# Attention weights' subtraction from GpSimd to VectorE, and later in the order

## The reference

```python
P = X @ W_in + b_in                     # 16 heads, each with Q, K, V, G of 64 columns
W = jnp.power(EPS + _cdist(Q, K), -2)   # EPS = 1e-4; _cdist: square root of the squared distance
W = W / (EPS + jnp.sum(W, axis=-1, keepdims=True))
A = jnp.einsum('hbts,hbse->hbte', W, V)
H = G * A                               # then @ W_out + b_out, residual, layer norm, sign-weight layer
```

## Time and profile before

| | |
|---|---|
| median of two runs | 5235.52 us (5234.5 to 5236.54) |
| profiled execution | 5237.27 us |
| its span on the slowest core | 5235.7 us |
| spans of the 8 cores | 5224.2 to 5235.7 us |
| first subtraction to the last | 347.2 to 4882.3 us |
| busy: PE, DVE, ACT, POOL | 52%, 24%, 58%, 42% of the span |
| mean granted TensorE clock | 0.653 of 2.4 GHz |

### The profile page before, as it was taken

The page is one execution under the profiler, slowest core; times in us unless marked ns, Lnnn a source line. Parts: engine busy times, 40 slices in busy tenths (PEclk is TensorE's granted clock), DMA queues, the critical chain, the costliest instruction groups (busy, mean ns, idle before and its releaser), DMA issues.

```text
span 5235.7 us, 45463 instructions; the slowest of 8 cores (5224.2 to 5235.7 us)
## 1 busy us (share of the span) xinstructions
PE 2736.5 (52%) x11472; PEld 1069.2 (20%) x11472; DVE 1273.1 (24%) x2118; ACT 3059.5 (58%) x2321; POOL 2176.6 (42%) x716
## 2 busy tenths in 40 slices
PE   1165555555555555546555555555465555544435
PEld 1122121212212121212122121212121221211112
DVE  4431312122121313131212213131312122120144
ACT  2127576675757575766667575757667675767200
POOL 0025444454545454444545354544445453545100
PEclk9976666666665656656666666666666666655657
DMA  2200000000000000000000000000000000000211
GB/s 77 63 7 1 9 2 6 5 1 9 2 9 1 9 2 10 1 7 3 2 9 1 9 2 9 1 9 2 7 4 1 9 2 9 1 1 1 97 32 65
DMA packets 42920, 64.15 MB, mean 12 GB/s; under 512 B 12992, under 2 KB 31424, under 8 KB 41664
## 3 DMA queue, kind: packets, MB, share of 16 engines
q1 hardware_dynamic: 36288, 61.03, 3.8%
q0 software_dynamic: 6400, 0.22, 0.1%
HBM read 50.39 MB, written 8.39 MB: 11 GB/s over the span
## 4 chain that ended last, share of the span: by engine, by line
PE 28%; POOL 25%; ACT 18%; issue 12%; DVE 9%; DMA 6%; DVEq 0%; POOLq 0%; SPq 0%; ACTq 0%
POOL wb L503 25%; PE pA L517 10%; ACT Ebc L498 9%; PE pp L333 8%; PE pS L480 5%; ACT Lb L489 5%; DMA Wst<-w_in 2%; DVE Wbf L318 2%; ACT Ea L495 2%; DMA rsrow<-A_sb 2%; DVE k2row L402 1%; PE pS L836 1%; PE pp L364 1%; PE pS L682 1%; PE pp L398 1%
## 5 line engine op out<-in xcount | busy, mean ns | idle before, releaser
L503 POOL TENSOR_TENSOR wb<-Ea,Ebc 128x2048 bf16<-128x2048 f32 x512 | 2080.9, 4064 | 2026.4 <-ACT Ebc L498 1634.8
L489 ACT ACTIVATE Lb<-pS 128x1024 f32<-128x1024 f32 x1024 | 1016.3, 1016 | 1093.5 <-PE pS L480 1090.9
L517 PE MATMUL pA<-wb,Vs 128*65 128x512 bf16 x2048 | 810.9, 538 | 1515.8 <-POOL wb L503 1515.8
L498 ACT ACTIVATE Ebc<-Lb 128x2048 bf16<-128x2048 f32 x512 | 972.7, 1900 | 92.9 <-POOL wb L503 92.0
L495 ACT ACTIVATE Ea<-Lb 128x2048 f32<-128x2048 f32 x512 | 977.8, 1910 | 77.3 <-ACT Lb L489 3.4
L480 PE MATMUL pS<-Qaug,Kaug 66*128 66x512 bf16 x2048 | 907.2, 546 | 213.8 <-ACT Lb L489 125.5
L517 PEld LDWEIGHTS pA<-wb,Vs 128*65 128x65 bf16 x2048 | 281.5, 138 | 2025.0 <-issue 1974.0
L333 PE MATMUL pp<-XnT,Wbf 128*64 128x512 bf16 x2048 | 598.5, 446 | 168.7 <-DVE Wbf L318 168.7
L371 DVE CAST Vs<-pp 128x64 bf16<-128x64 f32 x512 | 112.2, 224 | 1481.2 <-PE pp L364 1479.7
L364 PEld LDWEIGHTS pp<-Wbf,XnT 128*128 128x128 bf16 x4096 | 294.6, 130 | 240.1 <-issue 227.2
L333 PEld LDWEIGHTS pp<-XnT,Wbf 128*64 128x64 bf16 x2048 | 235.9, 125 | 521.6 <-issue 401.4
(11 more groups left out here) (83 smaller groups left out, 1164.3 us busy)
## 6 DMA issues: line engine op xcount, KB each, us to landing
xst<-x SPq DMA_DIRECT2D x32, 512.0 KB, 3.6
Wst<-w_in SPq DMA_DIRECT2D x128, 128.0 KB, 2.2
XT<-xT SPq DMA_DIRECT2D x8, 1024.0 KB, 16.9
y<-XT SPq DMA_DIRECT2D x32, 256.0 KB, 2.5
wst<-w_out SPq DMA_DIRECT2D x8, 512.0 KB, 4.5
wst<-w_ffn SPq DMA_DIRECT2D x8, 512.0 KB, 3.7
Kaug<-k2row POOLq DMA_DIRECT2D x128, 1.0 KB, 1.5
H<-Htmp SPq DMA_DIRECT2D x32, 64.0 KB, 1.9
```

The lines of the kernel that those rows point to most:

```text
L489: st("scalar", lambda e, ps=ps, sb=(r // 2) % 2, half=r % 2: e.activation(out=Lb[sb][:, half * 1024:half * 1024 + 1024], in_=pS[ps][:], fu ...
L498: st("scalar", lambda e, s=s: e.activation(out=Ebc[:], in_=Lb[s % 2][:], func=AF.Exp, scale=-1.5, bias=LN2EPS), waits=[(s_c3, s)], inc=s_c2)
L503: st("gpsimd", lambda e, s=s: e.tensor_tensor(out=wb[s % 2][:], in0=Ea[s % 2][:], in1=Ebc[:], op=ALU.subtract), waits=[(s_c2, 2 * s + 2), ...
L517: st("tensor", lambda e, hb=hb, stile=stile, ws=s % 2, half=r % 2, k=k, bk=bk: e.matmul(pAb[bk][0:65, :], Vs[hb][:, stile * 65:stile * 65 ...
```

## The change

The subtraction is given to VectorE instead of GpSimd, and it is emitted later in the region: behind the splice of the projection group (and behind A, the epilogue and `flush_w`) instead of right behind the exponentials. Operands, waits and semaphores stay as they are. It is emitted before the scores that open a new head.

```diff
     def emit_c3(s):
-        st("gpsimd", lambda e, s=s: e.tensor_tensor(
+        st("vector", lambda e, s=s: e.tensor_tensor(
             out=wb[s % 2][:], in0=Ea[s % 2][:], in1=Ebc[:], op=ALU.subtract),
            waits=[(s_c2, 2 * s + 2), (s_wcons, max(0, 4 * s - 4))], inc=s_c3)
...
         emit_c1(r)
         if r % 2 == 1:
             emit_c24(r // 2)
-            emit_c3(r // 2)
...
         if slot_in_head == 0:
             flush_w()
         splice(slot_in_head + 1, NQC * NREG)
+        if r % 2 == 1:
+            emit_c3(r // 2)
         if r + 1 < NTOT and nxt_head_start:
             emit_S(r + 1)
```

## The result

The changed kernel takes 5162.9 us (median of 7 runs, 5157.9 to 5179.5) where the kernel before takes 5235.6: a ratio of 0.986, 95% interval 0.984 to 0.987. That is 73 us, clear of noise and within the 2% that the forecast called no change. The profiled execution has a span of 5161.9 us on its slowest core.

A forecast was written before the change was run, and what follows sets the result against it. No engine is full; a loop of hand-overs sets the pace. Per head -9.0 + 8.8 + 1.8 + 1.9 - 2.7 = +0.8, 15 heads +12; last head -27.9, final subtraction -1.7: total -17.6, 5218, put at 5220 us (5090 to 5330).

The forecast's parts named there:

- The subtraction's price: One 2048-element subtraction on VectorE: 2.29 us, bounded by 2.04 and 2.42; with hand-over 2.56 instead of 4.22.
- V pairs: Region pairs 7 to 23 with V projection groups: 6.27 us each; eight with an epilogue 56.7 against 61.2, -9.0 a head.
- The epilogue's VectorE work: T1b and H, costed at nothing as hidden beside A and the first group; uncovered, 1.5 us in 60 pairs, 90 us.
- Wide pairs: Pairs 1 to 6 (Q, K) and 25 (G): most gaps cost one slow group, 10.2 us each, about 8.5 before.
- Norm pairs: Pairs 27 to 31, with square-and-row groups: 9.1 us each, five 45.5 against 43.6, +1.9 a head.
- The DMA behind the subtraction: Last pair to next head's scores: 2.3 us, or 4.2 if the DMA issue waits for the subtraction; 3.3 taken, -2.7.
- The head's start: Scores to pair 8: casts end 5.0 us earlier, but the first subtraction waits behind them; 106.5 against 97.7, +8.8.
- The last head: No projection groups, so ScalarE's floor sets most pairs: 200.4 us against 228.3, -27.9.
- head 0 behaves like the others: Head 0 has no wait for its successor's weights before or after, and loses the same in its wide groups.
- stay up: Rival: shorter TensorE gaps keep the clock high, seven wide pairs at 8.66 us, 180 us in all: 5040; chance 0.18.
- fall for whole pairs: Rival: one gap per pair keeps both groups and A at 1.2 GHz, wide pairs 12.8 us: 5475; chance 0.14.
- Face value: Rival: queue order costs nothing, so the subtraction's chain share shrinks by 572 us: 4660; chance 0.08, including cases between.

The follow-up runs named there:

- the early subtraction: Against the kernel before, the subtraction moved to VectorE but still emitted right behind the exponentials, ahead of the second group's evacuation: 4880.0 us, ratio 0.932.

## Why the prediction was right

The forecast was 5220 us, 5090 to 5330, within 2% at 0.64; measured were 5162.9 and -1.4%. The sum was 57 us too high: it forecast 15 us of gain and 73 came. Both lie under the 105 us that count as no change, so that the forecast held says little by itself, and the size of the gain was not foreseen. What bears the mechanism out are the steps:

**The subtraction's price.** Forecast 2.29 us, measured 2291 ns in 512 instructions. The bounds of 2.04 and 2.42 were not needed. The figure of the Trainium skill, "VectorE: DVE Perf Modes", The perf-mode tier table, 2293 ns for fp32, is met although one input is bf16.

**V pairs.** Forecast 56.7 us for eight, measured 56.3. Single ones are mostly 5.7 (the floor) or 6.3, and the pair with an epilogue is 13.2 to 13.5 on the mean (forecast 13.3). The epilogue's VectorE work, put at nothing, was next to nothing: the pair behind it takes 6.4.

**Wide pairs.** Forecast 10.2, measured 10.2, and more evenly than I thought: not "most gaps cost one slow group" but all except one of the 75 intervals from pair 1 to pair 6. Where the V pairs follow (6 to 7), the clock is still up and the pair takes 5.6 instead of 6.3; pair 25 is 11.1 instead of 10.4, as A is slow as well.

**Norm pairs.** Forecast 9.1, measured 9.1 to 9.3 (46.1 for five), link by link (columns as in the earlier trace rows):

```profile
2284.23 2.29 DVE L503 TENSOR_TENSOR wb<-Ea,Ebc 128x2048 bf16<-128x2048 f32 x1 [0.34 <-DVE k2row L402]
2284.59 1.91 ACT L495 ACTIVATE Ea<-Lb 128x2048 f32<-128x2048 f32 x1
2284.66 0.48 POOL L407 DMA_DIRECT2D Kaug<-k2row  x1 [2.57 <-DVEq L302]
2286.44 0.41 DVE L390 TENSOR_TENSOR KQsq<-Kaug 64x512 bf16<-64x512 bf16 x1
...
2289.24 0.68 DVE L402 CAST k2row<-pp 1x512 bf16<-1x512 f32 x1 [2.39 <-PE pp L398]
...
2292.30 0.68 DVE L402 CAST k2row<-pp 1x512 bf16<-1x512 f32 x1 [1.69 <-DMA Kaug<-k2row]
...
2293.31 2.29 DVE L503 TENSOR_TENSOR wb<-Ea,Ebc 128x2048 bf16<-128x2048 f32 x1 [0.34 <-DVE k2row L402]
```

**The DMA behind the subtraction.** I left open whether GpSimd can issue a DMA while VectorE subtracts, and took the middle of 2.3 and 4.2 us. The third row above settles it: issued at 2284.66 in 0.48 us, in the midst of the subtraction (2284.23 to 2286.52). So it is for 90 of the 192 row DMAs: their issues, 0.48 us each, lie within a subtraction, and the rows land 1.56 us (median) after the start of the issue, against 1.52 for the others. At the end of a head the scores came 2.1 us after the subtraction's start (2313.66 against 2311.60 and 2595.82 against 2593.72, both below). The middle was 1.2 us a head too high. The rule of the Trainium skill, "SBUF — State Buffer", SBUF: two separate sides, names for instructions with two SBUF inputs only a conflict with GpSimd instructions that read SBUF; I had stretched it to descriptor writes, and this trace does not bear that out. Nor are the casts of the earlier trace rows, with one input each, a case of two inputs; the squares (L390) are: 75 of 192 took over 1 us before, each beside a GpSimd subtraction, and none does now.

**The head's start: the term that was mis-sized.** I read it at head 8 and took it for all heads. There are two kinds. VectorE and SyncE in the changed kernel, at the start of head 7 and of head 8:

```profile
2311.60 2.29 DVE L503 TENSOR_TENSOR wb<-Ea,Ebc 128x2048 bf16<-128x2048 f32 x1 [0.57 <-DVE k2row L402]
...
2313.66 1.86 PE L480 MATMUL pS<-Qaug,Kaug 66*128 66x512 bf16 x4 [4.10 <-POOLq L418]
...
2319.34 14.23 SPq L314 DMA_DIRECT2D Wst<-w_in  x8
...
2335.41 0.29 DVE L318 CAST Wbf<-Wst 128x256 bf16<-128x256 f32 x1 [0.31 <-DMA Wst<-w_in]
...
2593.72 2.29 DVE L503 TENSOR_TENSOR wb<-Ea,Ebc 128x2048 bf16<-128x2048 f32 x1 [0.57 <-DVE k2row L402]
...
2595.82 1.87 PE L480 MATMUL pS<-Qaug,Kaug 66*128 66x512 bf16 x4 [4.14 <-POOLq L418]
...
2608.08 0.50 SPq L593 DMA_DIRECT2D H<-Htmp  x1
2608.66 10.05 SPq L314 DMA_DIRECT2D Wst<-w_in  x8
...
2620.65 0.29 DVE L318 CAST Wbf<-Wst 128x256 bf16<-128x256 f32 x1 [0.73 <-DMA Wst<-w_in]
```

After an odd head SyncE must first issue the DMA of Htmp, which waits for the whole epilogue, and the weight loads stand behind it: the last cast ends 25.1 us after the scores (forecast 24.6). After an even head there is no such DMA, the first two loads go out during the epilogue, and the last cast ends after 22.0. In the kernel before the difference is small: from pair 31 to pair 2 it took 46.9 us after an even head and 47.9 after an odd one, in the changed kernel it takes 45.0 and 48.2. In the kernel before, the GpSimd subtractions caught the early casts as well; at its head 7 two casts took 3.58 and 3.81 us. The edit takes the stretching away, and it is the early loads that profit. From pair 31 to 0 the mean is 25.9, not 27.9: 2.0 us a head, 28 us of the 57 (0.8 for the kind of head, 1.2 for the DMA above).

**The rest of the 57** (by means over heads, so rough). Pairs 0 to 8 were 1.5 us quicker than said (pairs 1 and 7: 10.7 and 5.6 against 11.3 and 6.3), the V pairs 0.9, pairs 24 to 31 slower by 1.2: 1.2 us over 15 heads, 18. And head 7, whose 286.8 I took for a head before, is 0.8 below the mean of 287.6: 11.

**The last head.** Forecast 200.4, measured 200.0: 28 intervals of 5.7 and three of 13.5.

**The sum by heads.** Head 0 lost 8.4 us, heads 1 to 13 won 40.0 together, head 14 won 16.5 and the last 28.4. Head 0's loss and head 14's gain are one thing: the block of casts, which lay behind a head's first subtraction and now lies ahead of it. That I had said head 0 behaves like the others was loose, but it cancels. The subtraction's 1.7 us at the very end did not come through: from the start of the last subtraction on it is 359.3 us against 357.5, with the output projection's matmuls at 433 ns against 406.

**The rivals.** The clock did not stay up and did not fall for whole pairs; in all but one of the intervals from pair 1 to pair 6 it cost one slow group. Face value (4660) was out of reach: even the early subtraction alone makes 4880. I had priced that rival by the subtraction's share of the chain; the 4800 that I expected of the early subtraction, from the loop's own links and ScalarE's floor, came nearer.

## What to carry to other kernels

When work moves to another engine, price the queue it lands in before the instruction: here the faster engine was worth 357 us (5236.6 to 4880.0) and the place behind two evacuations gave 283 of them back. Put the link of the loop that all else waits for ahead of the evacuations that have a second buffer, and put only the instruction that the next engine needs ahead of it (the square, not its cast). And look at each kind of loop turn, even and odd, before one of them is taken for all.

## What the runs showed of the hardware

- A VectorE subtraction of 2048 elements in 128 partitions, fp32 and bf16 in, bf16 out, takes 2.29 us; GpSimd takes 4.06.
- VectorE's casts from fp32 to bf16 and its bf16 squares were stretched from 0.29 to as much as 3.95 and from 0.42 to as much as 4.22 us beside a GpSimd subtraction; evacuations from PSUM were not (0.75 us before and after). Beside a VectorE subtraction, GpSimd's DMA issue stayed at 0.48 us.
- An idle gap of 2.7 us in a loop of 10.2 us brought TensorE from 2.4 to 1.2 GHz once a turn, in 74 of 75 turns; with 1.9 us of it filled the granted clock was 1.00, and the kernel with the useless matmuls was 99 us faster.
- Over most K pairs of the early subtraction, with gaps of 1.4 and 0.4 us in turn, the granted clock was 1.00. In norm pairs it was 0.50 before and after the change, in V pairs 0.62 and 0.63.
